# Graph attention layer: every third mirrored block transposed on VectorE and moved by on-chip transfers

## What is computed

```python
h = relu(layernorm(x))
cos = beta * (h @ h.T) / (norm(h) @ norm(h).T + 1e-7)
x = x + softmax(cos + (1 - adj) * -1e9, axis=1) @ h
h = relu(layernorm(x))
deg = clip(sum(adj, axis=1), 1)
x = x + h @ W_self + (adj @ h / deg) @ W_neigh
```

## Time and profile before

| | us |
|---|---|
| median of the runs | 495.34 |
| the profiled execution | 493.68 |
| its span, first to last instruction | 491.9 |
| TensorE busy | 466.6 |
| ScalarE busy | 284.9 |
| VectorE busy | 280.5 |
| GpSimd busy | 256.5 |
| queue q0 (GpSimd's), share of 16 engines | 25.3% |
| queue q1 (SP's), share of 16 engines | 23.7% |

### The profile page before, as it was taken

How to read it: one execution, slowest core, us unless ns; L and a number is a source line. 1 busy time by engine, 2 the same in 40 slices (tenths; PEclk the granted TensorE clock), 3 DMA queues, 4 the chain that set the end, 5 groups by cost and what they waited for, 6 DMA issues and landing times.

```text
span 491.9 us, 12305 instructions
## 1 busy us (share of the span) xinstructions
PE 466.6 (95%) x5200; PEld 390.6 (79%) x5200; DVE 280.5 (57%) x675; ACT 284.9 (58%) x425; POOL 256.5 (52%) x249
## 2 busy tenths in 40 slices
PE   1869999999999999999999999998999999999997
PEld 1737888888787887888878877886787888888886
DVE  6976756657566586565855675775766410122222
ACT  2998778775986767966698669777864100000000
POOL 3898767665875657755587468676662000000000
PEclk9999999999999999999999999999999999999999
DMA  8167776675787656976478746846500000000000
GB/s 249 21 79 167 136 124 142 111 157 76 133 161 134 128 80 110 181 131 141 71 120 179 121 66 133 166 67 98 72 8 1 13 12 23 23 23 23 23 22 22
DMA packets 31548, 46.06 MB, mean 94 GB/s; under 512 B 2560, under 2 KB 24320, under 8 KB 31488
## 3 DMA queue, kind: packets, MB, share of 16 engines
q0 software_dynamic: 10368, 9.44, 25.3%
q1 hardware_dynamic: 21120, 35.79, 23.7%
HBM read 71.43 MB, written 2.10 MB: 149 GB/s over the span
## 4 chain that ended last, share of the span: by engine, by line
PE 89%; DVE 5%; ACT 2%; POOL 1%; issue 1%; DMA 1%; SPq 0%; DVEq 0%
PE ps L1116 23%; PE ps L993 18%; PE ps L1004 10%; PE ps L1099 7%; PE ps L1096 7%; PE ps L1098 6%; PE ps L1071 5%; PE ps L1074 5%; PE ps L1073 5%; DVE adj_t L653 1%; DMA x_sb<-in_x_dram 1%; DVE word L798 1%; PE ps L1028 1%; POOL adj_t L398 1%; PE ps L1043 1%
## 5 line engine op out<-in xcount | busy, mean ns | idle before, releaser
L421 POOL TENSOR_TENSOR near<-word,adj_t 128x1024 f32<-128x1024 f32 x72 | 145.5, 2021 | 102.3 <-DVE word L798 98.8
L566 ACT ACTIVATE word<-ps,small 128x512 f16<-128x512 f32 x144 | 135.1, 938 | 79.2 <-PE ps L993 79.1
L798 DVE TENSOR_TENSOR word<-ps,word 128x512 f16<-128x512 f32 x144 | 105.8, 735 | 91.3 <-ACT ps L567 91.2
L1116 PE MATMUL ps<-table,adj_t 128*128 128x257 f16 x1024 | 114.6, 274 | 0.0
L993 PE MATMUL ps<-unit_t 128*128 128x512 f16 x432 | 107.0, 379 | 5.6 <-DVE word L798 3.9
L1116 PEld LDWEIGHTS ps<-table,adj_t 128*128 128x128 fp8e4 x1024 | 99.9, 98 | 13.6
L567 ACT ACTIVATE ps<-ps,small 128x512 f32<-128x512 f32 x144 | 107.0, 743 | 0.0
L1096 PE MATMUL ps<-table,near 128*128 128x129 f16 x576 | 102.6, 219 | 0.8 <-POOL near L421 0.7
L1099 PE MATMUL ps<-table,near 128*128 128x129 f16 x576 | 102.9, 222 | 0.0
L1098 PE MATMUL ps<-table,near 128*128 128x128 f16 x576 | 102.6, 219 | 0.0
L1071 PE MATMUL ps<-table,far 128*128 128x129 f16 x448 | 79.9, 219 | 0.2
(11 more groups left out here) (86 smaller groups left out, 440.2 us busy)
## 6 DMA issues: line engine op xcount, KB each, us to landing
stage<-in_adj_dram SPq DMA_DIRECT2D x56, 512.0 KB, 4.6
adj_t<-in_adj_dram POOLq DMA_DIRECT2D x72, 128.0 KB, 4.0
x_sb<-in_x_dram SPq DMA_DIRECT2D x4, 512.0 KB, 6.1
x_again<-in_x_dram SPq DMA_DIRECT2D x7, 256.0 KB, 5.9
out_dram<-x_sb SPq DMA_DIRECT2D x7, 256.0 KB, 2.9
far<-in_x_dram SPq DMA_DIRECT2D x1, 256.0 KB, 5.2
out_dram<-x_sb SPq DMA_DIRECT2D x1, 192.0 KB, 2.0
adj_t<-in_L_gnn_W_neigh_dram SPq DMA_DIRECT2D x1, 64.0 KB, 5.8
```

The costliest lines, as they stand in the source:

```text
L421: pool.tensor_tensor(ring(near, k), ring(word, k), adj_t[:, near_adj(k)], ALU.mult).then_inc(s_near, 1)
L566: act.activation(half(word16, k, c, 0, HIGH, TPS), score(k, c), ACT.Exp, bias=exp_bias, scale=exp_scale)
L798: dve.tensor_tensor(half(word16, k, c, 0, LOW, TPS), score(k, c), half(word16, k, c, 0, HIGH, TPS), ALU.subtract).then_inc(s_elo, 1)
L1116: return pe.matmul(ps[:, agg_bank(g, t), 0:TW], adj_t[:, at:at + P], tab(b), start=(b == 0), stop=(b == T - 1))
```

## The change

Seventeen of the 56 mirrored blocks no longer go through TensorE's transpose. `moved_pairs` picks them: from pair 8 on every third pair, while its step is below 5. For such a pair VectorE transposes the word in 32x32 blocks within each group of 32 partitions (`transpose_blocks`, in pass k - 1), and the SP queue moves the blocks between partition groups with 16 transfers of 32 partitions x 256 fp32 (`move_blocks`, placed between the loads for pairs k + 3 and the next). VectorE masks the moved word in pass k + 2 (`mask_moved`), and TensorE attends the block in pass k + 3 (`FAR_AT`), in the place of that pass's own block, which has itself been moved, or in a pass without one. `FAR_AT[k]` is the pair whose mirrored block is attended in pass k, `ORDER` their sequence.

```diff
+    MOVED, HOST = moved_pairs(PAIR)
+    NORMAL = [k for k in FAR if k not in MOVED]
+    GUEST = {HOST[k]: k for k in MOVED}
+    FAR_AT = [GUEST.get(k, k if k in NORMAL else None) for k in range(NP)]
...
+        packed32 = sb("packed32", [P, TILE], fp32)
+        slot = sb("moved_words", [P, TILE], fp32)
...
+            def move_blocks(k):
+
+                i = M_BEFORE[k]
+                sp.wait_ge(s_blocks, i + 1)
+                if i >= 1:
+                    sp.wait_ge(s_far_m, i)
+                for a in range(4):
+                    for q in range(4):
+                        sp.dma_start(slot[32 * a:32 * a + 32, 256 * q:256 * q + 256], packed32[32 * q:32 * q + 32, 256 * a:256 * a + 256]
+                                     ).then_inc(s_moved, 16)
+
...
                     load_far(k)
+                if k - 3 in MOVED:
+                    move_blocks(k - 3)
...
-                    if PAIR[k - 2][2]:
-                        act.wait_ge(s_turn, FAR_BEFORE[k - 1])
+                    if k - 2 in MOVED:
+                        act.wait_ge(s_blocks, M_BEFORE[k - 1])
+                    elif PAIR[k - 2][2]:
+                        act.wait_ge(s_turn, N_BEFORE[k - 1])
...
+            def transpose_blocks(k):
+
+                dve.wait_ge(s_elo, 2 * k + 2)
+                if M_BEFORE[k] >= 1:
+                    dve.wait_ge(s_moved, 256 * M_BEFORE[k])
+                dve.transpose(packed32[:, :].rearrange("p (a ct r) -> p a ct r", a=4, r=32),
+                              ring(word, k).rearrange("p (ct a r) -> p a ct r", a=4, r=32)).then_inc(s_blocks, 1)
+
+            def mask_moved(k):
+
+                m, i = FAR_BEFORE[k], M_BEFORE[k]
+                dve.wait_ge(s_moved, 256 * (i + 1))
+                dve.wait_ge(far_sem(m), m // 2 + 1)
...
+                dve.tensor_tensor(
+                    ring(far, at).rearrange("p (c t q r) -> p c t q r", c=2, t=TPS, q=4),
+                    slot[:, :].rearrange("p (q c t r) -> p c t q r", q=4, c=2, t=TPS),
+                    far_adj(k, adj_t).rearrange("p t (c q r) -> p c t q r", c=2, q=4), ALU.mult).then_inc(s_far_m, 1)
...
-                    if PAIR[k][2]:
-                        spill(k)
-                    if k + 1 < NP and PAIR[k + 1][2]:
+                    if FAR_AT[k] is not None:
+                        spill(FAR_AT[k])
+                    if k + 1 in NORMAL:
                         mask_far(k + 1)
+                    if k + 1 in GUEST:
+                        mask_moved(GUEST[k + 1])
+                    if k + 1 in MOVED:
+                        transpose_blocks(k + 1)
                     if k + 2 < NP:
                         low_part(k + 2, 1)
...
-                if PAIR[k][2]:
-                    attend_far(k)
+                if FAR_AT[k] is not None:
+                    attend_far(FAR_AT[k])
                 else:
                     attend_near(k)
-                if k + 1 < NP and PAIR[k + 1][2]:
+                if k + 1 in NORMAL:
                     turns(k + 1)
-                if PAIR[k][2]:
+                if FAR_AT[k] is not None:
                     attend_near(k)
...
+def moved_pairs(order):
+    far = [both for _, _, both in order]
+    moved, host = [], {}
+    k = 8
+    while k < len(order) and order[k][0] < 5:
+        if not far[k]:
+            k += 1
+            continue
+        at = k + 3
+        moved.append(k)
+        if order[at][0] >= 5:
+            at = min(i for i in range(at, len(order)) if not far[i])
+        host[k] = at
+        k = at
+    return moved, host
```

More of the change, by code:

```diff
@@ L22, in gnn_program @@
     FAR_BEFORE = [sum(m < k for m in FAR) for k in range(NP + 1)]
+    MOVED, HOST = moved_pairs(PAIR)
+    NORMAL = [k for k in FAR if k not in MOVED]
+    N_BEFORE = [sum(m < k for m in NORMAL) for k in range(NP + 1)]
+    M_BEFORE = [sum(m < k for m in MOVED) for k in range(NP + 1)]
+    GUEST = {HOST[k]: k for k in MOVED}
+    FAR_AT = [GUEST.get(k, k if k in NORMAL else None) for k in range(NP)]
+    ORDER = [k for k in FAR_AT if k is not None]
     FIRST = [min(k for k in range(NP) if PAIR[k][0] == s) for s in range(NS)] + [NP]
@@ L296, in gnn_program @@
         s_far = sem("far_words_masked")
+        s_blocks = sem("blocks_transposed_by_vector")
+        s_moved = sem("blocks_moved")
+        s_far_m = sem("moved_words_masked")
         s_pvd = sem("near_pair_attended")
@@ L746, in new_rows @@
                 if s >= 1:
-                    dve.wait_ge(s_spill, FAR_BEFORE[FIRST[s]])
+                    dve.wait_ge(s_spill, spilled(FIRST[s + 1]))
                 for b in range(2):
@@ L801, in mask_far, with spilled @@
             def mask_far(k):
-                m = FAR_BEFORE[k]
-                dve.wait_ge(s_turn, m + 1)
+                m, n = FAR_BEFORE[k], N_BEFORE[k]
+                dve.wait_ge(s_turn, n + 1)
                 dve.wait_ge(far_sem(m), m // 2 + 1)
-                if m >= 2:
-                    dve.wait_ge(s_pvt, m - 1)
+                at = ORDER.index(k)
+                if at >= 2:
+                    dve.wait_ge(s_pvt, at - 1)
                 dve.tensor_tensor(
-                    ring(far, m).rearrange("p (c t n) -> p c t n", c=2, t=TPS),
+                    ring(far, at).rearrange("p (c t n) -> p c t n", c=2, t=TPS),
                     ps[:, TURN:TURN + 2, :].rearrange("p c (t n) -> p c t n", t=TPS),
                     far_adj(k, adj_t).rearrange("p t (c n) -> p c t n", c=2), ALU.mult).then_inc(s_far, 1)
+            def transpose_blocks(k):
[8 more added lines that the diff above has]
+                dve.wait_ge(far_sem(m), m // 2 + 1)
+                at = ORDER.index(k)
+                if at >= 2:
+                    dve.wait_ge(s_pvt, at - 1)
+                dve.tensor_tensor(
+                    ring(far, at).rearrange("p (c t q r) -> p c t q r", c=2, t=TPS, q=4),
+                    slot[:, :].rearrange("p (q c t r) -> p c t q r", q=4, c=2, t=TPS),
+                    far_adj(k, adj_t).rearrange("p t (c q r) -> p c t q r", c=2, q=4), ALU.mult).then_inc(s_far_m, 1)
+            def spilled(k):
+                return len([j for j in FAR_AT[:k] if j is not None])
             def spill(k):
@@ L816, in spill @@
                 rows = x_v3[:, 2 * p:2 * p + 2, 0:D + 1]
-                dve.wait_ge(s_pvt, FAR_BEFORE[k] + 1)
+                dve.wait_ge(s_pvt, ORDER.index(k) + 1)
                 if s == 0:
@@ L820, in spill @@
                 else:
-                    if k == FIRST[s]:
-                        dve.wait_ge(s_spill, FAR_BEFORE[k])
+                    same = [j for j in FAR if PAIR[j][0] == s - 1 and PAIR[j][1] == p][0]
+                    if same in MOVED or ORDER.index(k) == min(ORDER.index(j) for j in FAR if PAIR[j][0] == s):
+                        dve.wait_ge(s_spill, ORDER.index(k))
                     dve.tensor_tensor(rows, two_rows(FAR_ACC), rows, ALU.add).then_inc(s_spill, 1)
@@ L997, in turn @@
             def turn(k, c, t):
-                m = FAR_BEFORE[k]
-                if c == 0 and t == 0 and m >= 1:
-                    pe.wait_ge(s_far, m)
+                n = N_BEFORE[k]
+                if c == 0 and t == 0 and n >= 1:
+                    pe.wait_ge(s_far, n)
                 if t == 0:
@@ L1062, in attend_far @@
                 s, p, _ = PAIR[k]
[L1063 to L1066, removed]
+                at, n = ORDER.index(k), N_BEFORE[k]
+                if k in MOVED:
+                    pe.wait_ge(s_far_m, M_BEFORE[k] + 1)
+                else:
+                    pe.wait_ge(s_far, n + 1)
+                if at >= 1:
+                    pe.wait_ge(s_spill, at)
                 for c in range(2):
@@ L1069, in attend_far @@
                         rows = s * TPS + t
-                        high, low = half(far16, m, c, t, HIGH), half(far16, m, c, t, LOW)
+                        high, low = half(far16, at, c, t, HIGH), half(far16, at, c, t, LOW)
                         pe.matmul(far_acc(c), high, tab(rows, D, TW), start=c == 0 and t == 0, stop=False,
@@ L1087, in attend_near @@
                     pe.wait_ge(s_spill, NT)
-                    pe.wait_ge(s_far, NT)
+                    pe.wait_ge(s_far, len(NORMAL))
                 elif first and s >= 1:
```

## The result

The changed kernel takes 574.58 us (median of four runs, 570.75 to 576.89) against 495.30 for the kernel before: ratio 1.161, 95% interval 1.157 to 1.165, so 79 us slower. The prediction said 503 us with a range of 482 to 520. The direction and the place were right, the size was a tenth of what came. The profiled execution of the changed kernel has a span of 571.0 us against 491.9.

The account below looks back on a forecast made before the run. The prediction took TensorE to bound the attention stage. Stalls of 25 us behind SP's queue against 15.0 saved gave +10, taken as +8 for double counting; 495.34 + 8 = 503.3, rounded to 503 us, range 482 to 520.

Parts of the forecast that it names:

- Saving, 15.0 us: TensorE in the attention stage: 17 moved pairs each take away 0.88 us of transposes that nothing covers.
- I take 0.38 each, 16 x 0.38 = 6.1 us: SP queue: time to issue one move's 16 transfers, priced by SP's issues of loads, ahead of the next mirrored load.
- four plain: Moves 11, 21, 27, 39, ScalarE converting the first load behind: TensorE stalls 1.5 us each for the low part, 6.0 together.
- four short: Moves 17, 33, 45, 55, where one of three passes has no mirrored block: TensorE stalls 3.8 us each, 15.2 together.
- two with a pair in between: Moves 30 and 42, with one pair more before ScalarE's late load: no stall, 0 us.
- seven of GpSimd's: Moves whose first late load GpSimd converts: conversion some 3 us late, mask ending near T + 14, no cost by itself.
- T + 15: About when TensorE needs GpSimd's mask of pair M+3; T is the end of VectorE's transpose of moved pair M.
- the 4 for the lateness after a stall: After a stalled cycle, a later transpose holds up exponentials, VectorE's queue and the next mirrored mask: 4 us in all.
- +42: Upper bound of the net change in us: 57 of stalls with slow issues and landings, less 15 saved.
- None of it is on the path by itself: VectorE's added transposes and mask delays, 26 us in passes it fills two thirds, were said not to set the time.
- 0.9 us in seven passes: VectorE's mask from two SBUF inputs, delayed by GpSimd's tile conversion: 0.9 us in about seven passes, bounds 0 and 2.0.
- the landing: Time for a move's last SBUF-to-SBUF transfer to land after issue: 2.9 us taken, between 1.6 and 5.9.

Follow-up runs that it names:

- e_psum_notr: e_psum_mask with VectorE's 17 transposes replaced by a memset of one column: 482.38 us, ratio 0.977 to the kernel before.
- e_psum_mask: e_none_early with the mask for moved pairs reading PSUM in place of the second SBUF tensor: 482.98 us, ratio 0.978 to the kernel before.
- e_add16: The kernel before plus 16 unused SBUF-to-SBUF transfers of 32 KB in SP's queue at each of the 17 places: 563.74 us, ratio 1.142.
- e_early16: The changed kernel with all sixteen transfers per move and the transpose put first in VectorE's pass: 562.88 us, ratio 1.136 to the kernel before.
- e_none_early: The changed kernel without its transfers, transpose first in VectorE's pass, two buffers for the transposed word: 487.83 us, ratio 0.985 to the kernel before.
- e_add16_dram: e_add16 with a DRAM tensor as the source of the extra transfers, same shape and size: 535.16 us, ratio 1.083 to the kernel before.
- e_bounce: The changed kernel with each move done by 5 transfers through DRAM, one store and four loads: 503.05 us, ratio 1.020 to the kernel before.
- e_add16_small: e_add16 with 32 columns in place of 256 per transfer (4 KB): 558.56 us, ratio 1.131 to the kernel before.

## Why the prediction was wrong

**Saving, 15.0 us: near.** With everything else out of the way (e_psum_notr) the kernel is 11.4 us faster than before; 3.6 of the 15 do not show. In e_psum_mask, TensorE's busy time is 13.5 us below that of the kernel before, and its idle time is 2.8 us above (28.1 for 25.3): it waits 15.7 us for the low part, 12.8 before, and 4.3 for the moved masks. Which of these takes the 3.6 was not tested.

**The term that failed: "I take 0.38 each, 16 x 0.38 = 6.1 us; bounds 16 x 0.33 = 5.3 and 16 x 0.48 = 7.7".** It measured 0.67 from issue to issue, 10.7 us per move. I priced a kind of transfer that the trace did not have by loads from DRAM and made their spread the bound; it was outside. The rest of the working bears the true value: with 4.6 us more, the prediction's stalls become 6.1 (four plain), 8.4 (four short), 4.2 (two with a pair in between, slack 0.4) and 3.6 (seven of GpSimd's, ready at T + 18.6 against T + 15). With the 4 for the lateness after a stall that is 96, less 15.0 is +81. That this is near the measured 79.3 is partly luck: the stalls alone make 92 of it, where e_add16 shows +70 for the queue, and the terms below were priced too low. The runs add up so: 70 for the queue, 12 for the late transpose (e_early16), 9 for what e_none_early leaves, less 15.0, is +76; 3 of the 79 stay open. The sensitivity was visible before the run: eight moves already had a stall and the other nine a slack of 0.4 to 1 us, so that each further microsecond of SP per move costs 10 us and more. From 8.0 to 10.7 us per move (e_add16_dram to e_add16) it was 28.6 us, some 10 for each. GpSimd's conversions, which were to cost nothing, wait 76.4 us for loads.

**The range.** My own upper bound was +42; I cut the range at +25. A term that is multiplied by 17 and has no row of its own deserved more than its neighbours' spread.

**"None of it is on the path by itself": wrong, twice.** The late transpose: I saw that the exponentials of pair M+2 wait for it and put 4 us for all such lateness; without any transfer it costs 11.4. The place in VectorE's queue, not the 1.24 us (taken: 1.2), is what costs. The mask beside GpSimd: I took 0.9 us in seven passes, 6 us of busy time, and called it hidden. Without transfers it is 4.8 us of busy time, most of it in five passes, and 3.6 to 4.9 us of the kernel's time, so the mechanism of the earlier trace rows was right and the overlap wrong. In the changed kernel itself, where the queue sets the pace, one mask of 17 is held up (2.09 us; mean 1.27). By the rows of the prediction TensorE wants the mask at t + 5.35 (4.05 + 1.3) and it ends at t + 4.6 alone and 5.4 beside GpSimd; I had worked out the start of that mask and never its deadline.

**Not priced at all: the clock.** TensorE runs the same 5064 instructions in e_psum_mask, where nearly all stalls are gone and the granted clock is 1.00, in 453.1 us of busy time; in the changed kernel it takes 474.5, 21 us more. The line of the mirrored attendance:

```profile
L1132 PE MATMUL ps<-table,far 128*128 128x129 f16 x448 | 88.8, 233 | 3.9 <-DVE far L857 3.2 <-DVE far L836 0.6
```

It is 79.9 us for the same 448 matmuls before and in e_psum_mask. The granted clock, 1.00 throughout before, is 0.94 over the span. Around one wait of TensorE, from 135.0 to 143.7 us, three windows of 4 us show it (after the span's length: TensorE's busy us and matmuls, and so on; the clock is the third number from the end):

```profile
136.00:140.00 4.00, 0.00 (x0) 0.00 (x0) 0.00 (x0) 0.00 (x0) 0.00 (x0) 0.79 0.94 223
144.00:148.00 4.00, 4.00 (x30) 3.01 (x29) 2.52 (x4) 4.00 (x6) 2.18 (x2) 0.50 0.47 144
152.00:156.00 4.00, 3.98 (x45) 3.00 (x43) 2.96 (x4) 4.00 (x7) 2.65 (x4) 1.00 0.70 87
```

The clock falls while TensorE is idle; right behind the wait TensorE works at the lower of its two levels (0.50, 1.2 GHz), 30 matmuls in a window where it starts 45 at the full clock. Up to 21 us of the 79 may be this second effect of the stalls. It is also part of the queue's 70 us (the clock of e_add16 is 0.97); it was read from the rows, not tested apart.

**Right:** the queue as the deciding mechanism, the conversions' waits for loads, SP's blocks of sixteen, the landing (2.5 us, taken 2.9), the durations of the mask when undisturbed and of the transpose (1.22 and 1.24), and that the moved word would be nearly in time (VectorE waited for it 3.4 us in three of 17 passes).

## What to carry to other kernels

An in-order DMA queue is a resource like an engine: before issues are added to it, list what stands behind them, each with its deadline, and price an issue of that very kind; if the trace has none, the bound has to be wide. Fewer and larger transfers won here even with twice the bytes and a detour through DRAM. When a wait is moved from one engine to another (here the release of a buffer from TensorE to VectorE), put the releasing instruction into idle time ahead of the queue, and when a pass gets shorter, work out the deadlines in it again.

## What the runs showed of the hardware that I had not expected

SP's issue of a transfer from SBUF to SBUF takes 0.59 us, from DRAM to SBUF 0.42 in the same place and shape, and neither bytes (4 to 128 KB) nor rows (32 or 128) change it much. The store of 512 KB from SBUF to DRAM (e_bounce) takes 0.33.

VectorE can stand in one instruction while several of GpSimd's go by, also in an instruction with a single tensor input. The scaling of the weights, 0.28 us in the kernel before, took 4.23 us in the changed one, beside three GpSimd instructions that followed each other without a gap while it caught up; VectorE's first, then GpSimd's:

```profile
94.01 4.23 DVE L882 TENSOR_SCALAR w_parts<-adj_t 128x256 f16<-128x256 f32 x1
```

```profile
93.97 1.06 POOL L465 TENSOR_SCALAR adj_t<-stage 128x1024 uint8<-128x1024 f32 x1
94.99 2.02 POOL L446 TENSOR_TENSOR near<-word,adj_t 128x1024 f32<-128x1024 f32 x1
96.96 1.12 POOL L413 TENSOR_TENSOR table<-adj_t,table 128x512 f16<-128x512 f32 x1
```

It ended at 98.24, after the last of them. In e_add16, e_add16_small and e_early16 the same instruction takes 4.22 to 4.24 us, in e_add16_dram 3.70, in the other runs 0.27 to 0.28. That GpSimd is what holds it is read from these rows, not tested. The Trainium skill (SBUF — State Buffer, "SBUF: two separate sides") tells of such an exclusion, for VectorE's instructions with two SBUF inputs or in a two-port performance mode, and for the length of the one instruction that started first; here three went by before VectorE was through, and no run shows in which mode it ran.
